# The first layer's softmax division by way of DRAM, and half of its bias product on GpSimd

## Chip, cores and metric

The kernel runs on one core of one Trainium2 chip. The metric is the device time of one execution in microseconds. The kernel before takes 1226.16 us (median of 3 runs, 1225.27 to 1228.61).

## What is computed

The input is 32 images of 16 by 16 tokens with 256 channels, all in float32. Two layers follow each other, each of the form x = x + attention(groupnorm(x)). The change touches the first layer alone, which is shifted-window attention: 4 windows of 64 tokens an image, 16 heads of 16 channels.

```python
q = (xw @ Wq.T).reshape(-1, N, HEADS, d).transpose(0, 2, 1, 3)      # k alike, v with a bias
qn = q / jnp.maximum(jnp.linalg.norm(q, axis=-1, keepdims=True), 1e-12)   # kn alike
logits = jnp.einsum('bhnd,bhmd->bhnm', qn, kn) * scale
logits = logits + 16.0 * jax.nn.sigmoid(bias)
lg = jnp.where(mask[None, :, None], -jnp.inf, lg)
scores = jax.nn.softmax(logits, axis=-1)
o = jnp.einsum('bhnm,bhmd->bhnd', scores, v)
z = o @ Wo.T + bo
```

## The kernel before

In the code the first layer is `layer0`. It is a software pipeline over the 32 images, written out for each engine by itself. The helper `pipeline` takes a list of stages with lags: in step s an engine runs each stage of its list, in the list's order, for image s + lag. Engines meet only at semaphores, so each engine works through its list in order, and an instruction that waits holds up all behind it on that engine.

Steps 4 to 25 are a hardware loop (`Fori`) of 11 rounds with two steps in each; steps -6 to 3 and 26 to 32 are written out in full. So ahead of each even step from 4 to 24 each engine jumps: it enters the loop, or goes back to its top. It does not jump ahead of an odd step.

What a step does in the kernel before, with the lines of its profile:

- TensorE (PE): `scores` of image s into psG (L365, L372), `project_v` of s+1 (L408), `output` of s-1 (L422), `bounds` of s+1 into psG (L389, L396), `turn` of s+2 (L433), `sums` of s, the softmax's denominators (L443), `weigh` of s, the weights times v (L457), `project` of s+3 in two halves (L469), `groups` of s+4 (L484), `turn_c` of s+1 (L476), and `spread_sums` of s (L491), one matmul that spreads 64 columns of inverted sums over 512.
- ScalarE (ACT): two `exponent` halves from psG into the weights (L575), `copy_v` (L567), `copy_z` of s-1 (L582), `normalize` of s+3 (L615), `copy_qk` (L589, L592), `copy_o` (L600), two `square` halves of s+3 (L559), `copy_c` (L605).
- VectorE (DVE): `add_bias`, the product of the exponentials with the exponential of the bias, in two halves (L698), `unit_qk` (L778), two `take_max` (L771), `invert_sums` (L681), `spread_blocks` (L686), statistics (L786, L793 to L717), two `norms` (L705), `outputs` of s (L676), which divides by the sums, and then `seeds` and `roots` (L727 to L763), a Newton iteration for reciprocal roots: 3 small instructions and then 9, nearly all of them waiting for the one in front. L763 is the last of them and writes `shift`.
- GpSimd (POOL): only `residual` of s-1, four additions into X (L828). The queue of SyncE (SP) issues the load of image s+6 (L301).

`newton` counts the nine instructions of `roots`, `biased` the bias products, `sums_done` and `r_done` the sums and their inverses, `o_out` the weighted values copied out, `o_done` the divided ones that `output` waits for. ebias, the weights and rdx (which holds the spread inverses) lie in SBUF; psG, psA and psE are PSUM.

## Time and profile before

| | before |
|---|---|
| median of 3 runs | 1226.16 us |
| profiled execution | 1223.74 us |
| its span | 1222.0 us |
| PE busy | 1153.9 us (94%) |
| DVE busy | 945.0 us (77%) |
| ACT busy | 639.0 us (52%) |
| POOL busy | 209.5 us (17%) |

The profiled execution took 1223.74 us, of which the span of the engines' instructions is 1222.0 us. The first layer lies between 0 and about 537 us of the span; its 32 steps begin with the L365 matmuls. "Idle before" is time in which an engine had nothing running, and the name behind the arrow is what released it as far as the profile can tell.

### The profile page before, as it was taken

The page shows a single profiled execution, that of the slowest core. Times are in us where ns is not written, and L with a number is a line of the kernel's source. Part 1 is how long each engine was busy: PE and PEld are TensorE (multiplying, and loading weights), DVE is VectorE, ACT ScalarE, POOL GpSimd, SP SyncE. Part 2 cuts the span into 40 slices and gives each one's busy share as a digit, 9 for nine tenths or more (in the row PEclk, how much of TensorE's full clock was granted, in tenths as well). Part 3 has the DMA queues.
Part 4 walks back from the last instruction along what each step waited for, and adds up shares of the span by engine and source line. Part 5 has one row for each costly group of instructions (what it writes and reads, how often), then busy time and mean ns, then how long its engine had stood idle before and what let it go on. Part 6 is the DMA issues. An engine that isn't in the chain of part 4 may idle for free.

```text
span 1222.0 us, 50870 instructions
## 1 busy us (share of the span) xinstructions
PE 1153.9 (94%) x21404; PEld 842.1 (69%) x21404; DVE 945.0 (77%) x1687; ACT 639.0 (52%) x1051; POOL 209.5 (17%) x271
## 2 busy tenths in 40 slices
PE   6899999999999999958899999999999999999983
PEld 3677777777777777736677777777777777777752
DVE  5588888888888898744577878787787878778753
ACT  4365566666566665422555555555555555555540
POOL 0001111111111111120212212221221222222120
PEclk9799999999999999988999999999999999999987
DMA  2000000000000000010023122222312222231222
GB/s 90 17 21 21 20 17 17 17 17 17 17 17 17 17 10 3 4 40 1 11 54 71 41 65 44 61 45 60 70 40 65 44 61 45 59 69 40 66 45 70
DMA packets 180189, 46.04 MB, mean 38 GB/s; under 512 B 146308, under 2 KB 179350, under 8 KB 180118
## 3 DMA queue, kind: packets, MB, share of 16 engines
q1 hardware_dynamic: 178056, 43.76, 15.2%
q10 hardware_dynamic: 2064, 1.26, 0.4%
q8 instruction: 56, 0.92, 0.3%
q14 instruction: 13, 0.11, 0.0%
HBM read 27.56 MB, written 17.30 MB: 37 GB/s over the span
## 4 chain that ended last, share of the span: by engine, by line
PE 44%; DVE 6%; issue 3%; SPq 0%; ACT 0%; DMA 0%; POOL 0%; POOLq 0%; DVEq 0%
PE psG L1063 14%; PE psA L1105 8%; PE psA L1121 6%; PE psG L1085 6%; PE psE L1154 5%; PE psA L1133 5%; DVE of L1261 3%; DVE sums L1256 2%; PE psG L1072 2%; DVE cm L1230 1%; PE psE L1144 1%; DMA sums<-totals 0%; SPq L1012 0%; ACT probs L1176 0%; POOL probs L1292 0%
## 5 line engine op out<-in xcount | busy, mean ns | idle before, releaser
L1230 DVE TENSOR_REDUCE cm<-psG 128x4 f32<-128x1024 f32 (+1 forms) x192 | 235.0, 1224 | 132.2 <-PE psG L1085 132.2
L1176 ACT ACTIVATE probs<-psG 128x1024 f32<-128x1024 f32 x192 | 196.4, 1023 | 143.4 <-PE psG L1063 143.0
L1063 PE MATMUL psG<-stack 32*128 32x256 f32 (+1 forms) x2048 | 222.6, 345 | 9.7 <-DVE cm L1230 6.6
L1292 POOL TENSOR_SCALAR_AFFINE_SELECT probs<-probs 128x1024 f32<-128x1024 f32 x128 | 139.2, 1099 | 517.6 <-ACT probs L1176 517.6
L1072 PE MATMUL psG<-stack 32*128 32x256 f32 (+1 forms) x2048 | 220.1, 342 | 4.3 <-DVE cm L1230 2.4
L1063 PEld LDWEIGHTS psG<-stack 32*128 32x128 f32 x2048 | 152.5, 188 | 68.0 <-DVE cm L1230 27.6
L1072 PEld LDWEIGHTS psG<-stack 32*128 32x128 f32 x2048 | 149.8, 185 | 7.0 <-DVE cm L1230 3.3
L828 POOL TENSOR_TENSOR X<-X,probs 128x96 f32 (+5 forms) x128 | 64.8, 536 | 467.8 <-ACT probs L582 467.8
L1121 PE MATMUL psA<-xh,wqk 128*128 128x256 f32 x512 | 126.2, 391 | 5.5 <-DVE xh L1267 5.5
L469 PE MATMUL psA<-probs,xh 128*128 128x512 f32 x256 | 128.7, 630 | 1.9 <-ACT xh L615 1.6
L1256 DVE RECIPROCAL sums<-sums 128x128 f32<-128x128 f32 x128 | 115.7, 929 | 10.4 <-DMA sums<-totals 10.4
L1121 PEld LDWEIGHTS psA<-xh,wqk 128*128 128x128 f32 x512 | 95.6, 197 | 17.7 <-DVE xh L1267 6.2
L1190 ACT ACTIVATE stack<-psA,at_row,own 128x256 f32<-128x256 f32 x128 | 65.1, 561 | 68.7 <-DVE stack L1236 68.7
L1105 PE MATMUL psA<-probs,va 128*32 128x256 f32 (+1 forms) x2048 | 97.8, 332 | 0.9 <-POOL probs L1292 0.9
L575 ACT ACTIVATE probs<-psG 128x1024 f32<-128x1024 f32 x64 | 62.0, 1021 | 69.8 <-PE psG L372 69.8
L698 DVE TENSOR_TENSOR probs<-probs,ebias 128x1024 f32<-128x1024 f32 x64 | 77.9, 1220 | 13.4 <-ACT probs L575 13.2
L1105 PEld LDWEIGHTS psA<-probs,va 128*32 128x32 f32 x2048 | 57.8, 110 | 37.2 <-issue 14.3
L1154 PE MATMUL psE<-of,wo 128*128 128x256 f32 x256 | 67.4, 408 | 16.7 <-DVE of L1261 15.0
L559 ACT ACTIVATE probs<-psA 128x512 f32<-128x512 f32 x64 | 38.1, 597 | 84.3 <-PE psA L469 84.3
L771 DVE TENSOR_REDUCE cm<-psG 128x16 f32<-128x1024 f32 x64 | 75.3, 1219 | 7.6 <-PE psG L396 6.7
L469 PEld LDWEIGHTS psA<-probs,xh 128*128 128x128 f32 x256 | 44.6, 194 | 38.8 <-issue 36.2
L1154 PEld LDWEIGHTS psE<-of,wo 128*128 128x128 f32 x256 | 48.2, 198 | 30.6 <-DVE of L1261 24.2
(132 smaller groups left out, 1890.0 us busy)
## 6 DMA issues: line engine op xcount, KB each, us to landing
X<-in_xr SPq DMA_DIRECT2D x32, 256.0 KB, 2.7
scratch_heads<-ots SPq DMA_DIRECT2D x128, 64.0 KB
raw<-scratch_heads SPq DMA_DIRECT2D x32, 256.0 KB
sums<-totals SPq DMA_DIRECT2D x64, 128.0 KB
out<-X SPq DMA_DIRECT2D x32, 256.0 KB, 3.1
totals<-ots SPq DMA_DIRECT2D x128, 4.0 KB
probs<-in_wqk ACTq DMA_DIRECT2D x1, 512.0 KB, 4.4
wqk<-in_wqk SPq DMA_DIRECT2D x1, 512.0 KB, 3.6
```

The costliest lines, as they stand in the source:

```text
L469: last = nc.tensor.matmul(A[t][:], xh[i.k][:, c, t * P:(t + 1) * P], wqk[:, c, :], start=(c == 0), stop=(c == CT - 1))
L698: nc.vector.tensor_tensor(both, both, bias.unsqueeze(2).to_broadcast([P, 4, WINDOWS, WTOK]), ALU.mult).then_inc(biased, 1)
L771: nc.vector.reduce_max(cm[:, t, :].rearrange("p (r s) -> p r s", s=COL)[:, :, 0:SLOTS], banks.rearrange("p r (s k) -> p r s k", k=WTOK), A ...
L1063: last = nc.tensor.matmul(G[:, at:at + b.size], km[i.k][own_rows(r), o, e, b.keys_of(o) * P:(b.keys_of(o) + 1) * P], qm[i.k][own_rows(r), ...
L1072: nc.tensor.matmul(G[:, at:at + b.size], qm[j.k][own_rows(r), o, e, b.queries_of(o) * P:(b.queries_of(o) + 1) * P], km[j.k][own_rows(r), o ...
L1105: last = nc.tensor.matmul(A[0 if o else 2][COL * c:COL * (c + 1), to:to + b.size], va[i.k][:, b.keys_of(o), TILE_HEADS * o + 2 * r + e, :] ...
L1121: last = nc.tensor.matmul(A[o][:, n * TOKENS:(n + 1) * TOKENS], wqk[:, c, n * CH + o * P:n * CH + (o + 1) * P], xh[i.k][:, c, :], start=(c ...
L1154: last = nc.tensor.matmul(E[:, o * TOKENS:(o + 1) * TOKENS], wo[:, f, o * P:(o + 1) * P], of[:, f, :], start=(f == 0), stop=(f == CT - 1))
L1176: nc.scalar.activation(weights[i.k][:, b.weights_at:b.weights_at + 1024], G[:, 0:1024], ACT.Exp).then_inc(exp_done, 1)
L1230: nc.vector.reduce_max(slots, scores, AX_X).then_inc(max_done, 1)
L1256: nc.vector.reciprocal(piece, piece).then_inc(r_done, 1)
L1292: nc.gpsimd.affine_select(out=diagonal, in_=diagonal, compare_op=ALU.is_ge, fill=0.0, base=0, pattern=[[0, QUADS], [0, 2], [sign, P]], cha ...
```

## The change

The spreading of the inverted sums leaves TensorE and VectorE. `spread_blocks` and `spread_sums` are gone. SyncE's queue instead writes the 128x64 inverses to a DRAM buffer (`put_inverses`, 32 KB) and reads them back broadcast into rdx (`get_inverses`, 256 KB, each head's row to 16 partitions). `outputs` now reads rdx from SBUF, not from PSUM, waits for that read, and moves from the end of step s to the front of step s+1.

The second half of the bias product moves to GpSimd (`add_bias` in the gpsimd block, on weight columns 1024 to 2047). It waits for both exponentials and for `newton` of image s+3, that is for the `roots` that VectorE ran last. From step 30 on there is no such wait.

The orders change too: on TensorE `bounds` comes ahead of `output`, `weigh` ahead of `sums`, `turn_c` ahead of the second half of `project`; on ScalarE `normalize` comes ahead of `copy_z` and `copy_c` ahead of the second `square`.

```diff
--- before.py
+++ after.py
+    inverses = nc.dram_tensor("inverses", [2, P, WTOK], F32).ap()
...
+            def put_inverses(i):
+                wait_alone(sp, r_done, i.count(1))
+                wait_alone(sp, got[i.k], i.plus(-2).dmas(1))
+                sp.dma_start(inverses[i.k], rd[:, :]).then_inc(put[i.k], 16)
+
+            def get_inverses(i):
+                wait_alone(sp, put[i.k], i.dmas(1))
+                wait_alone(sp, o_done, i.plus(-1).count(1))
+                by_head = inverses[i.k].rearrange("(g u n) q -> g u (n q)", u=2, n=8)[:, 0]
+                sp.dma_start(rdx, by_head.unsqueeze(1).to_broadcast([8, DIM, 512])).then_inc(got[i.k], 16)
+
+            pipeline(sp, images, [(load, 6), (put_inverses, 0), (get_inverses, 0)], LAGS, once={-5: small_inputs, -4: regions})
...
             def sums(i):
 
-                wait(pe, biased, i.count(2))
                 wait(pe, z_out, i.plus(-1).count(2))
+                wait(pe, r_done, i.plus(-1).count(1))
                 for n in range(8):
...
             def weigh(i):
 
-                wait(pe, v_out, i.count(2))
-                if i.plus(1).among(images):
-                    wait(pe, v_out, i.plus(1).count(2))
+                for n in range(2):
+                    wait(pe, biased[n], i.count(1))
+                wait(pe, v_out, (i.plus(1) if i.plus(1).among(images) else i).count(2))
                 for o in range(CT):
...
-            def spread_sums(i):
-
-                wait(pe, rdx_done, i.count(1))
-                nc.tensor.matmul(E[:, :], spread, rdx, start=True, stop=True).then_inc(spread_done, 1)
-
-            pipeline(pe, images, [(scores, 0), (project_v, 1), (output, -1), (bounds, 1), (turn, 2), (table_read, 0), (sums, 0), (weigh, 0),
-                                  (lambda i: project(i, 0), 3), (groups, 4), (lambda i: project(i, 1), 3), (turn_c, 1),
-                                  (spread_sums, 0)], LAGS, once={-3: hide_early, -2: hide_late, -1: tabulate})
+            pipeline(pe, images, [(scores, 0), (project_v, 1), (bounds, 1), (output, -1), (turn, 2), (weigh, 0), (table_read, 0), (sums, 0),
+                                  (lambda i: project(i, 0), 3), (groups, 4), (turn_c, 1), (lambda i: project(i, 1), 3)], LAGS, once={-3: hide_early, -2: hide_late, -1: tabulate})
...
-                                   (copy_v, 1), (copy_z, -1), (normalize, 3), (copy_qk, 2), (bias_across, 1),
-                                   (copy_o, 0), (lambda i: square(i, 0), 3), (lambda i: square(i, 1), 3), (bias_within, 1), (copy_c, 1)], LAGS, once={-3: rectify_early, -2: rectify_late, -1: open_table})
+                                   (copy_v, 1), (normalize, 3), (copy_z, -1), (copy_qk, 2), (bias_across, 1),
+                                   (copy_o, 0), (lambda i: square(i, 0), 3), (bias_within, 1), (copy_c, 1), (lambda i: square(i, 1), 3)], LAGS, once={-3: rectify_early, -2: rectify_late, -1: open_table})
...
             def outputs(i):
 
-                wait(dve, spread_done, i.count(1))
+                wait_alone(dve, got[i.k], i.dmas(1))
                 wait(dve, o_out, i.count(1))
                 raw = ot[:, :, :].rearrange("p o t -> p (o t)")
-                nc.vector.tensor_tensor(raw, E[:, :], raw, ALU.mult).then_inc(o_done, 1)
+                nc.vector.tensor_tensor(raw, rdx, raw, ALU.mult).then_inc(o_done, 1)
 
             def invert_sums(i):
                 wait(dve, sums_done, i.count(QUADS))
-                wait(dve, rdx_done, i.plus(-1).count(1))
+                wait_alone(dve, put[1 - i.k], i.plus(-1).dmas(1))
                 nc.vector.reciprocal(rd[:, :], E[:, 0:WTOK]).then_inc(r_done, 1)
 
-            def spread_blocks(i):
-                wait(dve, r_done, i.count(1))
-                wait(dve, spread_done, i.plus(-1).count(1))
-                nc.vector.tensor_tensor(rdx.rearrange("p (n q) -> p n q", q=WTOK), rd[:, :].unsqueeze(1).to_broadcast([P, 8, WTOK]),
-                                        block_of[:, :].unsqueeze(2).to_broadcast([P, 8, WTOK]), ALU.mult).then_inc(rdx_done, 1)
-
-            def add_bias(i, part):
-
-                wait(dve, exp_done, i.count(2, part + 1))
-                if part == 0:
-                    wait(dve, tab_in, 32)
-                    wait(dve, a_tab2, 4 * QUADS)
-                both = (weights[i.k][:, part * 1024:(part + 1) * 1024]
-                        .rearrange("p (n w q) -> p n w q", w=WINDOWS, q=WTOK))
-                bias = ebias[:, 2 * part:2 * part + 2, :, :].rearrange("p r o q -> p (r o) q")
+            def add_bias(i):
+
+                wait(dve, exp_done, i.count(2, 1))
+                wait(dve, tab_in, 32)
+                wait(dve, a_tab2, 4 * QUADS)
+                both = weights[i.k][:, 0:1024].rearrange("p (n w q) -> p n w q", w=WINDOWS, q=WTOK)
+                bias = ebias[:, 0:2, :, :].rearrange("p r o q -> p (r o) q")
                 nc.vector.tensor_tensor(both, both, bias.unsqueeze(2).to_broadcast([P, 4, WINDOWS, WTOK]),
-                                        ALU.mult).then_inc(biased, 1)
+                                        ALU.mult).then_inc(biased[0], 1)
...
-            pipeline(dve, images, [(lambda i: add_bias(i, 0), 0), (unit_qk, 2), (prepare_bounds, 2), (invert_table, 1), (lambda i: add_bias(i, 1), 0), (lambda i: take_max(i, 0), 1), (lambda i: take_max(i, 1), 1),
-                                   (invert_sums, 0), (spread_blocks, 0), (stats_next, -1), (stats_first, 5),
-                                   (variances, 4), (lambda i: norms(i, 0), 3), (lambda i: norms(i, 1), 3), (outputs, 0),
+            pipeline(dve, images, [(outputs, -1), (unit_qk, 2), (add_bias, 0), (prepare_bounds, 2), (invert_table, 1), (lambda i: take_max(i, 0), 1), (lambda i: take_max(i, 1), 1),
+                                   (invert_sums, 0), (stats_first, 5), (stats_next, -1),
+                                   (variances, 4), (lambda i: norms(i, 0), 3), (lambda i: norms(i, 1), 3), 
                                    (scale_ready, 4), (seeds, 4, 1), (roots, 4, 1)], LAGS,
...
-            pipeline(pool, images, [(residual, -1)], LAGS)
+            def add_bias(i):
+
+                wait(pool, exp_done, i.count(2))
+                if i.plus(3).among(images + 1):
+                    wait(pool, newton, i.plus(3).count(NEWTON))
+                if first(i):
+                    pool.wait_ge(tab_in, 32)
+                    pool.wait_ge(a_tab2, 4 * QUADS)
+                both = weights[i.k][:, 1024:2048].rearrange("p (n w q) -> p n w q", w=WINDOWS, q=WTOK)
+                bias = ebias[:, 2:4, :, :].rearrange("p r o q -> p (r o) q")
+                nc.gpsimd.tensor_tensor(both, both, bias.unsqueeze(2).to_broadcast([P, 4, WINDOWS, WTOK]),
+                                        ALU.mult).then_inc(biased[1], 1)
+
+            pipeline(pool, images, [(add_bias, 0), (residual, -1)], LAGS)
```

On VectorE, at the top of the hardware loop and just ahead of it (the same instructions stand ahead of a return to the top). Before, the roots' last instruction and the jump were followed by the bias product:

```order
L763 SCALAR_TENSOR_TENSOR shift<-gs,rs_y 128x2
L126 UNCONDITIONAL_BRANCH
L126 ISA
L698 TENSOR_TENSOR probs<-probs,ebias 128x1024 [waits a_tab2,tab_in,exp_done]
L93 ISA
L93 REGISTER_ALU [waits newton]
L778 TENSOR_TENSOR probs<-psA,rs_y 128x512 [waits turned]
L778 TENSOR_TENSOR probs<-psA,rs_y 128x512
L93 REGISTER_ALU
L698 TENSOR_TENSOR probs<-probs,ebias 128x1024 [waits exp_done]
```

And in the changed kernel:

```order
L754 SCALAR_TENSOR_TENSOR shift<-gs,rs_y 128x2
L126 UNCONDITIONAL_BRANCH
L126 ISA
L93 REGISTER_ALU [waits got1]
L675 TENSOR_TENSOR ot<-probs,ot 128x512 [waits o_out]
L93 ISA
L93 ISA [waits newton]
L769 TENSOR_TENSOR probs<-psA,rs_y 128x512 [waits turned]
L769 TENSOR_TENSOR probs<-psA,rs_y 128x512
L93 REGISTER_ALU
L689 TENSOR_TENSOR probs<-probs,ebias 128x1024 [waits a_tab2,tab_in,exp_done]
```

`outputs` (L675) has come to the front, with two SBUF inputs, and one bias product of two is left, behind `unit_qk` (L769).

On TensorE, the middle of a step in the loop, before:

```order
L422 MATMUL psE<-ot,probs 128x2x8x8 [waits o_done]
L422 MATMUL psE<-ot,probs 128x2x8x8 x7
L389 MATMUL psG<-stack 64x128 [waits gn_chain,exp_done,qk_out]
L389 MATMUL psG<-stack 64x128 x31
L396 MATMUL psG<-region_keys,region_queries 64x256 x16
L93 REGISTER_ALU
L433 MATMUL psA<-ident,probs 128x128 [waits qkn_done]
L433 MATMUL psA<-ident,probs 128x128 x7
L443 MATMUL psE<-probs 32x64 [waits z_out,biased]
L443 MATMUL psE<-probs 32x64 x31
L457 MATMUL psA<-probs,vw 32x64 [waits v_out]
L457 MATMUL psA<-probs,vw 32x64 x31
```

And in the changed kernel:

```order
L400 MATMUL psG<-stack 64x128 [waits gn_chain,exp_done,qk_out]
L400 MATMUL psG<-stack 64x128 x31
L407 MATMUL psG<-region_keys,region_queries 64x256 x16
L433 MATMUL psE<-ot,probs 128x2x8x8 [waits o_done]
L433 MATMUL psE<-ot,probs 128x2x8x8 x7
L93 REGISTER_ALU
L444 MATMUL psA<-ident,probs 128x128 [waits qkn_done]
L444 MATMUL psA<-ident,probs 128x128 x7
L468 MATMUL psA<-probs,vw 32x64 [waits v_out,biased1,biased0]
L468 MATMUL psA<-probs,vw 32x64 x31
L454 MATMUL psE<-probs 32x64 [waits r_done,z_out]
L454 MATMUL psE<-probs 32x64 x31
```

`bounds` (L400) now comes directly behind `project_v`, `output` (now L433) behind it, and `weigh` (L468) is the one that waits for both bias products.

## Rows read from the trace of the kernel before

**Rows 1.** Timeline of PE, one step: start us, length us, engine, line, operation.

```profile
255.76 1.53 PE L365 MATMUL psG<-stack 32*64 32x64 f32 x124
...
259.39 2.05 PE L422 MATMUL psE<-ot,probs 128*128 128x128 f32 x16
261.37 1.19 PE L389 MATMUL psG<-stack 32*64 32x128 f32 x63
...
262.73 1.10 PE L433 MATMUL psA<-ident,probs 128*128 128x128 f32 x8
263.75 1.10 PE L443 MATMUL psE<-probs 128*32 128x64 f32 x64
...
267.64 1.96 PE L469 MATMUL psA<-probs,xh 128*128 128x512 f32 x4
269.44 0.38 PE L476 MATMUL psG<-ident,cm 128*128 128x128 f32 x2
269.66 1.02 PE L491 MATMUL psE<-probs 128*128 128x512 f32 x2
270.74 1.53 PE L365 MATMUL psG<-stack 32*64 32x64 f32 x124
...
285.62 1.53 PE L365 MATMUL psG<-stack 32*64 32x64 f32 x124
```

**Rows 2.** Timeline of ACT, the same step and the next.

```profile
257.65 1.94 ACT L575 ACTIVATE probs<-psG 128x1024 f32<-128x1024 f32 x2 [2.02 <-PE psG L372]
...
272.71 1.94 ACT L575 ACTIVATE probs<-psG 128x1024 f32<-128x1024 f32 x2 [2.20 <-PE psG L372]
```

**Rows 3.** Timeline of DVE, the same step and the next.

```profile
259.25 0.15 DVE L763 SCALAR_TENSOR_TENSOR shift<-gs,rs_y 128x2 f32<-128x2 f32 x1
259.34 1.23 DVE L698 TENSOR_TENSOR probs<-probs,ebias 128x1024 f32<-128x1024 f32 x1
260.48 1.28 DVE L778 TENSOR_TENSOR probs<-psA,rs_y 128x512 f32<-128x512 f32 x2
261.68 1.22 DVE L698 TENSOR_TENSOR probs<-probs,ebias 128x1024 f32<-128x1024 f32 x1
...
270.27 0.69 DVE L705 TENSOR_REDUCE rs<-probs 128x32 f32<-128x512 f32 x1 [0.94 <-ACT probs L559]
...
271.47 0.22 DVE L727 SCALAR_TENSOR_TENSOR rs<-rs 128x66 f32<-128x66 f32 x1
...
274.14 0.15 DVE L763 SCALAR_TENSOR_TENSOR shift<-gs,rs_y 128x2 f32<-128x2 f32 x1
274.75 1.23 DVE L698 TENSOR_TENSOR probs<-probs,ebias 128x1024 f32<-128x1024 f32 x1 [0.46 <-ACT probs L575]
```

**Rows 4.** L828, the last image: count, duration ns min/median/max, forms.

```profile
L828 POOL TENSOR_TENSOR X<-X,probs x4: 249/383/785, 534.4 to 535.9; 128x96 f32<-128x96 f32 x2, 128x288 f32<-128x288 f32 x1, 128x32 f32<-128x32 f32 x1
```

**Rows 5.** L1261, all of the second layer, columns alike.

```profile
L1261 DVE TENSOR_TENSOR of<-raw,sums x32: 691/1116/1205, 624.3 to 1214.1; 128x512 f32<-128x512 f32 x32
```

**Rows 6.** Timeline of POOL and DVE around one L1261 (second layer).

```profile
623.81 1.10 POOL L1292 TENSOR_SCALAR_AFFINE_SELECT probs<-probs 128x1024 f32<-128x1024 f32 x1
624.34 1.11 DVE L1261 TENSOR_TENSOR of<-raw,sums 128x512 f32<-128x512 f32 x1
```

**Rows 7.** DMA issues: engine, operation, count, KB each, median us to landing.

```profile
X<-in_xr SPq DMA_DIRECT2D x32, 256.0 KB, 2.7
...
ebias<-probs ACTq DMA_DIRECT2D x2, 64.0 KB, 2.2
```

**Rows 8.** Timeline of all engines at the end of the first layer.

```profile
528.17 0.56 DVE L681 RECIPROCAL rd<-psE 128x64 f32<-128x64 f32 x1 [1.30 <-PE psE L443]
...
531.42 2.05 PE L422 MATMUL psE<-ot,probs 128*128 128x128 f32 x16 [0.78 <-DVE ot L676]
533.51 0.84 ACT L582 ACTIVATE probs<-psE,bz 128x256 f32<-128x256 f32 x2 [3.85 <-PE psE L422]
534.42 1.68 POOL L828 TENSOR_TENSOR X<-X,probs 128x288 f32<-128x288 f32 x4 [6.00 <-ACT probs L582]
```

26 lines of the change are left out of this document (9 added, 17 removed).

## Prediction

> **What bounds the kernel now.** The first thing to read is the timeline of TensorE over one step [rows 1], starts only, since the matmuls overlap. Scores start at 255.76, 270.74 and 285.62: two steps in 29.86 us, 14.93 each, and each block of matmuls starts as the last one's ends. In the first layer's loop TensorE shows no pause, so time taken out of its list is won, as long as nobody else becomes late. The pieces that I need, as differences of starts: scores and project_v together 3.63 (255.76 to 259.39), output 1.98, bounds 1.36, turn 1.02, then sums, weigh, the first half of project and groups together 3.89 (263.75 to 267.64), the second half of project 1.80, turn_c 0.22, spread_sums 1.08 (269.66 to 270.74).
>
> Then VectorE [rows 3]. From the second project's start (267.64) it goes by ScalarE's square to the second L705 at 270.27 (2.63 us), and from seeds at 271.47 to the end of L763, the last of the roots, at 274.29 (2.82); between them stands outputs (L676). The next thing to see is the difference of two neighbouring steps. In the first, L698 starts at 259.34, 0.06 before L763 ends. In the second VectorE is idle for 0.46 us and L698 starts at 274.75. The row blames the exponential, but its first half, which is what L698 waits for, was done by about 273.7 [rows 2], before L763 started. What lies between is the jump to the top of the loop. So in every even step of the loop VectorE comes 0.46 us late to what follows the roots. Before, this costs nothing, since sums has slack.
>
> Last, who can disturb whom in SBUF. L1261 in the second layer multiplies two SBUF tiles of 128x512 on VectorE. Alone it takes 691 ns, the minimum; the median is 1116 [rows 5]. The timeline shows the reason: GpSimd's L1292 runs from 623.81 to 624.91, L1261 starts at 624.34 and ends at 625.45, 0.54 after GpSimd [rows 6]. So VectorE stood still until GpSimd's whole instruction was done, and then did its 512 elements. The Trainium skill, "SBUF — State Buffer", section "Who interferes with whom", states this as an exclusive lock on a shared pair of ports, which the one that starts first keeps for a whole instruction. By that rule a VectorE instruction with one SBUF input isn't touched; the rule speaks against this change, and the row agrees with its first part.
>
> **The change, part by part.** I count from x, the start of the second half of project in the step before; the steady period is x to x. T is the start of scores.
>
> 1. *TensorE's list.* spread_sums goes: -1.08. T is now x + 1.80. But bounds moved ahead of output, and bounds overwrites the psG that the exponentials read. They start T + 1.89 (255.76 to 257.65) and take 1.94 [rows 2], so bounds can start at T + 3.83 plus about 0.12 for the signal, 3.95, where TensorE arrives at T + 3.63. The new wait is 0.32. By TensorE alone a step is 14.93 - 1.08 + 0.32 = 14.2. I take weigh's arrival from it: T + 3.95 + 1.36 + 1.98 + 1.02 = T + 8.31 = x + 10.1. From weigh to the next x: 3.89 + 0.22 = 4.11.
>
> 2. *spread_blocks* and one half of add_bias leave VectorE (the half at 261.68 is 1.22 long [rows 3]). VectorE isn't what TensorE waits for before, so this alone is worth nothing.
>
> 3. *The roots.* Without outputs ahead of them, seeds wait for L705's end: 0.69 + 0.03. L763 ends at x + 2.63 + 0.72 + 2.82 = x + 6.17. Call this u.
>
> 4. *GpSimd's product.* The trace has none of this size. From 32 elements in 249 ns and 288 in 785 undisturbed [rows 4] an element costs 2.09 ns, so 1024 elements cost 2.32 us. The lower bound is L1292's 1.10 us for as many elements with one input [rows 6]; I take 2.32, from the same operation with two inputs. With 1.10 the even steps below are 1.22 us shorter and the odd ones 0.1, some 15 us in all (1218). The upper bound is the 383 ns of the 96-element pieces taken per element, 4.1, fixed share and all; it would put 1.8 us on each step. I keep it for the range with little weight, since the 288 elements rule it out (they would take 1.15). The Trainium skill, "GPSIMD Engine Reference", section "Elementwise — side-by-side cycle accounting", gives about 2.6 cycles an element for two inputs, by which it would be an estimated 2.2 us and the sum below some 2 us less.
>
> 5. *Odd steps, and steps written out: VectorE first.* outputs starts at about u - 0.06 as L698 did, and ends at u + 0.62 by L1261's 0.69 undisturbed. It has two SBUF inputs now. GpSimd's product, released at u, stands until then and ends 2.32 - 0.15 later (0.15 is what L1261 had behind it before it was stopped, 0.69 - 0.54), at u + 2.79. unit_qk reads PSUM and one small SBUF tile. No row here shows such an instruction against GpSimd; I take it as running meanwhile, since only its second input is in SBUF, and price the contrary as a rival. add_bias, two SBUF inputs, would be ready at u + 1.7 and is held until u + 2.79, then takes 1.08 more: u + 3.87. With 0.1 for signals weigh may start at x + 10.1 to x + 10.2, just as TensorE arrives. The period is 10.17 + 4.11 = 14.3, against a mean of 14.93 before: -0.63.
>
> 6. *Even steps of the loop: GpSimd first.* After the jump outputs cannot start before u + 0.46. GpSimd already sits at its wait for newton, and starts 0.07 after a release (534.35 to 534.42 [rows 8]). It holds SBUF until u + 2.39. outputs ends 0.54 later, at u + 2.93. TensorE's output needs it, and turn and weigh stand behind output: it starts at x + 6.17 + 2.93 + 0.06 = x + 9.16, not at x + 7.1, and weigh at + 1.98 + 1.02 = x + 12.16. (The bias half ends at u + 2.93 - 0.09 + 1.20 + 1.23 = u + 5.27 = x + 11.45, hidden under it.) The period is 12.16 + 4.11 = 16.27: +1.34.
>
> 7. *The two transfers.* By the nearest rows, a write of 64 KB landed in 2.2 us and a read of 256 KB from DRAM in 2.7 [rows 7]: 4.9 with both. The inverses are ready about x - 1.4 (weigh and sums 1.93 behind W, invert 0.55 after), so rdx is there near x + 3.7 with the queue's own delays, and outputs wants it at x + 6.1. Hidden by 2.4 us a step. The loads of X are issued behind the read and have a whole step. At the layer's end nothing hides them: from the start of the last L681 to output it was 3.25 us (528.17 to 531.42 [rows 8]); now 0.55 + 4.9 + 0.69 + 0.1 = 6.2, and sums stand behind weigh and GpSimd's 2.32 instead of VectorE's 1.2. That is 3 + 2, of which the two last steps, free of VectorE work behind them, give something back. I take +4, between +2 and +6.
>
> The sum: 11 even steps x 1.34 = +14.7; 11 odd steps and 7 written-out full ones x -0.63 = -11.3; end +4. Together +7.4. Against the profiled 1223.7 us this is 1231.1; the median of the runs stands 2.4 above the profiled one, so I predict 1233.5.
>
> **Rivals.**
>
> *VectorE is never the one held* (0.17): the jump is faster in the new code, or GpSimd takes the ports more than 0.46 us after its release. For it: nothing in the trace shows a two-input product of GpSimd issued against a VectorE one at the same moment. Against: the 0.46 against the 0.07. All 29 steps then win 0.63, the end costs 4: -14, 1212. This is the case on the other side, and it decides at u + 0.46.
>
> *GpSimd first in the odd steps too* (0.09): if the wait for the transfer delays outputs by over 0.15 us. Then 11 more steps move from 14.30 to 16.27, +21.7: 1255.
>
> *unit_qk is held as well* (0.06), having an SBUF input. By the rule of the same page it isn't. Where VectorE goes first, unit_qk would start at u + 2.79 and add_bias end 1.2 later than above, 18 steps x 1.25 = +22: 1256.
>
> *The transfers are late* (0.04): from 7.3 us for both on, each microsecond costs one a step. With 8 us, 29 x 0.7 = +20: 1253.
>
> *Nothing nets out* (0.04), some cost and gain sized otherwise: 1226.
>
> **How the numbers follow.** The main case has 0.60. Its own range is 1228 to 1239: the even steps by 0.3 (3 us), the others by 0.2 (4 us), the end by 2. What a measurement can tell from no change is 0.3%, 3.7 us. The main case is slower than that in 0.8 of its weight, the same in 0.17. With the rivals: slower 0.48 + 0.09 + 0.06 + 0.04 = 0.67, faster 0.17 + 0.02 = 0.19, same 0.14. The range 1211 to 1248 leaves out the cases around 1255 and half of the faster one's low side.
>
> **What would show it.** Scores' starts alternating near 14.3 and 16.3 us in the loop. In even steps GpSimd's product 2.3 us long, then outputs with over 2 us on the clock, and TensorE idle by some 2 us before output, released by VectorE. In odd steps outputs of 0.7, a GpSimd product of about 2.9, and add_bias of over 2 us. TensorE idle 0.3 before bounds. No wait for a transfer before step 31, and 5 us of it there. What would make me wrong: equal steps, a GpSimd product of 3 us or more undisturbed, or VectorE waiting for a DMA inside the loop.

## The result, and the profile after

The changed kernel takes 1265.68 us (median of 4 runs, 1255.7 to 1273.61), the kernel before 1227.38 us on the same chip (4 runs, 1225.27 to 1228.95). The ratio is 1.031, 95% interval 1.022 to 1.040. The forecast was slower, and it was slower, but 1265.7 lies outside the range of 1211 to 1248: the cost is 38 us where 7 were forecast.

The profiled execution of the changed kernel took 1271.29 us, 5.6 more than the median. Its span is 1269.2 us against 1222.0, 47.2 more, so the parts below add up to more than the 38. Cut at the first scores of a step, it divides like this:

| stretch | before | after | difference |
|---|---|---|---|
| start to step 4 | 120.0 | 124.2 | +4.2 |
| steps 4 to 25, the hardware loop | 329.7 | 361.4 | +31.7 |
| steps 26 to 30 | 71.1 | 68.3 | -2.8 |
| step 31 to the end | 701.1 | 715.3 | +14.2 |

The first view is the timeline of TensorE, as in [rows 1], for steps 14 to 16.

```profile
287.68 1.53 PE L376 MATMUL psG<-stack 32*64 32x64 f32 x124
...
289.42 1.97 PE L419 MATMUL psA<-wv,xh 128*64 128x128 f32 x32
291.64 1.19 PE L400 MATMUL psG<-stack 32*64 32x128 f32 x63 [0.26 <-ACT probs L580]
...
295.24 2.05 PE L433 MATMUL psE<-ot,probs 128*128 128x128 f32 x16 [2.17 <-DVE ot L675]
...
298.10 1.10 PE L468 MATMUL psA<-probs,vw 128*32 128x64 f32 x64
...
304.05 1.53 PE L376 MATMUL psG<-stack 32*64 32x64 f32 x124
...
312.56 1.10 PE L468 MATMUL psA<-probs,vw 128*32 128x64 f32 x64 [0.31 <-DVE probs L689]
...
320.33 1.12 PE L376 MATMUL psG<-stack 32*64 32x64 f32 x81 [1.75 <-issue]
323.09 0.96 PE L376 MATMUL psG<-stack 32*64 32x64 f32 x41 [1.64 <-issue]
...
324.51 3.68 PE L419 MATMUL psA<-wv,xh 128*64 128x128 f32 x32
```

Step 14 (even) is 16.37 long. `output` (L433) comes 2.17 us late and the row names VectorE's `outputs`. Step 15 shows only 0.31 ahead of `weigh`. Then the scores of step 16 start at 320.33, 1.75 us after TensorE ran dry, and stop once more for 1.64, both times on "issue": nothing that the profile shows was waited for. After these pauses L419 takes 3.68 us in place of 1.97. VectorE and GpSimd in the same steps, with the counterparts of [rows 3]:

```profile
292.06 0.15 DVE L754 SCALAR_TENSOR_TENSOR shift<-gs,rs_y 128x2 f32<-128x2 f32 x1
292.29 2.35 POOL L832 TENSOR_TENSOR probs<-probs,ebias 128x1024 f32<-128x1024 f32 x1 [8.88 <-DVE shift L754]
292.61 2.58 DVE L675 TENSOR_TENSOR ot<-probs,ot 128x512 f32<-128x512 f32 x1 [0.40 <-issue]
295.11 1.28 DVE L769 TENSOR_TENSOR probs<-psA,rs_y 128x512 f32<-128x512 f32 x2
296.31 1.21 DVE L689 TENSOR_TENSOR probs<-probs,ebias 128x1024 f32<-128x1024 f32 x1
...
308.52 0.68 DVE L675 TENSOR_TENSOR ot<-probs,ot 128x512 f32<-128x512 f32 x1
308.68 2.75 POOL L832 TENSOR_TENSOR probs<-probs,ebias 128x1024 f32<-128x1024 f32 x1 [8.51 <-DVE shift L754]
309.12 1.28 DVE L769 TENSOR_TENSOR probs<-psA,rs_y 128x512 f32<-128x512 f32 x2
310.32 2.19 DVE L689 TENSOR_TENSOR probs<-probs,ebias 128x1024 f32<-128x1024 f32 x1
```

This is the alternation that the prediction described. In the even step the jump costs VectorE 0.40, GpSimd is first, and `outputs` lasts until 295.19, 0.55 after GpSimd's end. In the odd step `outputs` is first (0.68), and then L689 is the one held. L769, with one input in PSUM, takes 1.28 in both.

What the prediction didn't have shows in the windows, one line a step (steps 14, 15, 16 and 18), with the busy time of TensorE, its weight loads, VectorE, ScalarE and GpSimd, and then TensorE's granted clock, the DMA engines' share and GB/s:

```profile
287.67:304.05 16.38, 13.95 (x422) 10.83 (x421) 13.62 (x30) 9.09 (x17) 4.06 (x5) 1.00 0.12 33
304.05:320.33 16.28, 14.00 (x421) 10.84 (x421) 13.40 (x32) 9.76 (x18) 4.46 (x5) 1.00 0.15 36
320.33:338.54 18.21, 16.57 (x421) 13.08 (x421) 11.03 (x29) 8.61 (x16) 4.54 (x5) 0.81 0.13 34
...
354.68:372.69 18.01, 15.58 (x421) 12.46 (x421) 13.62 (x30) 9.20 (x17) 4.06 (x5) 0.91 0.12 30
```

The second line is an odd step of 16.28: 14.5 and the 1.75 of pause at its end. The third has a clock of 0.81, which means a part of the step at 1.2 GHz in place of 2.4. And the page's table of DMA queues has one line that changed, the fetching of instructions, first before and then after:

```profile
q8 instruction: 56, 0.92, 0.3%
```

```profile
q8 instruction: 83, 1.36, 0.4%
```

Each packet is a block of 16 KB of instructions. 27 more are three bursts of nine, and their times in the trace begin at 217.0, 315.9 and 415.5, each 0.6 to 0.7 us after TensorE's sequencer, which runs ahead of the matmuls, has jumped back to the top of the loop (216.36, 315.30 and 414.76). In the kernel before there is none between 145 and 448 us, that is from the first round, which brings the loop's code in, to the end of the last. So the loop's instructions, once fetched, normally stay on the chip; in the changed kernel they are now and then fetched anew.

### The profile page after: what moved, and what is told of

It reads as the page before. It is cut to its first block, busy times and chain, and to the rows that moved or that the text cites. A ratio compares the mean times of both kernels' runs of the same rounds, so it can differ in the third digit from the quotient of the medians.

```text
span 1269.2 us, 50942 instructions
## 1 busy us (share of the span) xinstructions
PE 1148.0 (90%) x21340; PEld 850.2 (67%) x21340; DVE 926.2 (73%) x1620; ACT 641.4 (51%) x1051; POOL 282.0 (22%) x303
## 4 chain that ended last, share of the span: by engine, by line
PE 43%; DVE 6%; issue 3%; SPq 1%; ACT 0%; DMA 0%; POOL 0%; POOLq 0%; DVEq 0%
PE psG L1067 13%; PE psA L1109 7%; PE psA L1125 6%; PE psG L1089 5%; PE psE L1158 5%; PE psA L1137 4%; DVE of L1265 3%; DVE sums L1260 2%; PE psG L1076 2%; DVE cm L1234 1%; PE psE L1148 1%; DMA sums<-totals 0%; SPq L1016 0%; ACT probs L1180 0%; SPq L1020 0%
## 5 line engine op out<-in xcount | busy, mean ns | idle before, releaser
L1180 ACT ACTIVATE probs<-psG 128x1024 f32<-128x1024 f32 x192 | 196.6, 1024 | 143.3 <-PE psG L1067 142.9
L832 POOL TENSOR_TENSOR probs<-probs,ebias 128x1024 f32<-128x1024 f32 x32 | 82.3, 2573 | 344.2 <-DVE shift L754 212.3
L433 PE MATMUL psE<-ot,probs 128*128 128x128 f32 x512 | 72.3, 299 | 30.2 <-DVE ot L675 30.2
L433 PEld LDWEIGHTS psE<-ot,probs 128*128 128x128 f32 x512 | 65.7, 208 | 37.1 <-DVE ot L675 34.4
L762 DVE TENSOR_REDUCE cm<-psG 128x16 f32<-128x1024 f32 x64 | 75.0, 1211 | 11.2 <-PE psG L407 11.2
L1109 PEld LDWEIGHTS psA<-probs,va 128*32 128x32 f32 x2048 | 57.8, 110 | 37.2 <-issue 14.3
L419 PE MATMUL psA<-wv,xh 128*64 128x128 f32 x1024 | 74.5, 301 | 7.6 <-issue 7.6
```

Of the source, the lines that this page charges most:

```text
L433: last = nc.tensor.matmul(dst[:, t], wo[:, f, o * P:(o + 1) * P], ot[:, f, t * P:(t + 1) * P].rearrange("p (ww rr c) -> p ww rr c", ww=2, ...
L832: nc.gpsimd.tensor_tensor(both, both, bias.unsqueeze(2).to_broadcast([P, 4, WINDOWS, WTOK]), ALU.mult).then_inc(biased[1], 1)
L1109: last = nc.tensor.matmul(A[0 if o else 2][COL * c:COL * (c + 1), to:to + b.size], va[i.k][:, b.keys_of(o), TILE_HEADS * o + 2 * r + e, :] ...
L1180: nc.scalar.activation(weights[i.k][:, b.weights_at:b.weights_at + 1024], G[:, 0:1024], ACT.Exp).then_inc(exp_done, 1)
```

## The experiments

Fifteen kernels were run, each timed against the kernel before on its own chip (in the four groups of runs its medians were 1241.52, 1230.6, 1233.42 and 1225.5 us; the first and the third are of one chip at two times). Lengths of steps and loops are those of one profiled execution each. The theory: the prediction's steps are right in the loop, and what it left out are re-fetched instructions with the lower clock behind them. The rivals: the held `outputs`, the product or the transfers cost more than was counted. Each expectation spells out what they mean for its run, and in the later ones the letters stand for what they name there.

### Two tries to move the loop that moved nothing

```diff
                 pe.wait_ge(made, MADE)
+                for _ in range(20):                # and 128
+                    pe.nop(nofuse=True)
                 for q in range(HALF):
```

> The changed kernel with 20 empty instructions on TensorE ahead of its loop, nothing else. In the changed kernel TensorE's instruction blocks (16 KB each) are fetched again in the loop, nine of them every third round, from 217, 316 and 416 us on; before, none is fetched inside the loop. Its loop starts 17 instructions earlier than that of before. Theory A (where the loop lies against the 16 KB blocks decides whether it is fetched again): with the loop's start back at the old place there are no fetches in the loop, no odd step of 16 or 18 us, odd steps 14.5 and even ones 16.4, and the kernel takes about 1240 us (1234 to 1246). Rival B (the fetches come from TensorE's longer waits or from the traffic of the two transfers): the fetches stay, 1255 to 1273 us.

> The same with 128 empty instructions, half a block. Theory A: the loop's 1710 instructions end 128 further into the last block; either no fetches (about 1240 us) or more of them (every round, over 1280 us), in any case another pattern than nine blocks every third round. Rival B: unchanged, 1255 to 1273 us with the same fetches.

Measured 1271.67 us (pad20), ratio 1.025 (1.018 to 1.031), and 1270.08 (pad128), ratio 1.024 (1.017 to 1.031). The trace counts as many instructions up to each fetch as in the changed kernel, so the empty instructions didn't reach the instruction stream. These are two repeats of the changed kernel and say nothing on the loop's place. What they do show is that the fetches vary: four bursts (187.7 to 423.7 us) in one, three in the other, with a clean stretch from 311 to 435 in which steps are 14.46 and 16.37.

### GpSimd's product behind outputs

```diff
             def add_bias(i):                       # on GpSimd
                 if i.plus(3).among(images + 1):
-                    wait(pool, newton, i.plus(3).count(NEWTON))
+                    wait(pool, o_done, i.plus(-1).count(1))
```

> The changed kernel, but GpSimd's product waits for outputs of image s-1 (o_done) where it waited for the roots. Theory (in even steps GpSimd takes SBUF ahead of outputs): outputs is 0.7 us long in every step, TensorE waits for it no more, GpSimd's product ends 3.1 to 3.7 us after the roots and the bias half on VectorE is held until then; even steps 15.1 in place of 16.4, odd steps 14.5 to 14.7, 11 to 14 us less than the changed kernel's 1266, with the fetches as they are: about 1253. Rival (outputs is late for another reason, the rdx transfer): outputs still ends 2.9 us after the roots in even steps, no gain.

Measured 1238.1 us (hold_outputs), ratio 0.998 (0.995 to 1.001). The timeline of an even step:

```profile
304.75 0.69 DVE L675 TENSOR_TENSOR ot<-probs,ot 128x512 f32<-128x512 f32 x1 [0.40 <-issue]
305.53 2.36 POOL L832 TENSOR_TENSOR probs<-probs,ebias 128x1024 f32<-128x1024 f32 x1 [10.15 <-DVE ot L675]
306.56 2.41 DVE L689 TENSOR_TENSOR probs<-probs,ebias 128x1024 f32<-128x1024 f32 x1
```

The same jump of 0.40, but `outputs` is back to 0.69. Steps are 15.23 and 14.68, the loop 329.6, and no fetch and no halved clock falls into it. So the order of the two engines is what makes the even steps long, and the transfers don't. The fetches went as well, with not one TensorE instruction changed; the expectation had left them in.

### Both halves of the product on VectorE, transfers kept

```diff
-  pipeline(dve, images, [(outputs, -1), (unit_qk, 2), (add_bias, 0), ...
+  pipeline(dve, images, [(outputs, -1), (unit_qk, 2), (lambda i: add_bias(i, 0), 0), (lambda i: add_bias(i, 1), 0), ...
-  pipeline(pool, images, [(add_bias, 0), (residual, -1)], LAGS)
+  pipeline(pool, images, [(residual, -1)], LAGS)
```

> The changed kernel with both halves of the bias product on VectorE (behind unit_qk), none on GpSimd; the two transfers stay. Theory: no VectorE instruction is held by GpSimd; even steps 15.1 (the jump's 0.46 us and the longer VectorE list), odd ones 14.5, about 1253 us with the fetches as they are, 1228 without. Rival (the transfers cost the step): even steps stay at 16.4 and the kernel above 1260.

Measured 1236.99 (product_vector), ratio 0.997 (0.994 to 1.000), steps 15.29 and 14.67, loop 330.2, no fetches. The transfers by themselves cost nothing in the loop. At the end they do: from step 31 to the last `output` it is 18.1 us against 10.5, and 707.9 from step 31 on against 701.1.

### The product on GpSimd, without transfers

```diff
   # the kernel before without VectorE's second half, and on GpSimd the changed kernel's add_bias
...
-                wait(pe, biased, i.count(2))
+                for n in range(2):
+                    wait(pe, biased[n], i.count(1))
-  pipeline(pool, images, [(residual, -1)], LAGS)
+  pipeline(pool, images, [(add_bias, 0), (residual, -1)], LAGS)
```

> The kernel before with the second half of the bias product on GpSimd alone, held until the roots as in the change; sums are spread by TensorE, outputs stays ahead of the roots. Theory (the lock costs only because outputs, which TensorE wants early, stands behind the product): in even steps the VectorE half is about 3.4 us long on the clock, sums waits for nothing, steps 14.9, ratio 0.995 to 1.005. Rival (GpSimd's product costs in itself): over 1.01.

Measured 1228.05 (product_only), ratio 0.997 (0.994 to 1.000); steps 14.88 and 14.98, loop 329.8, no fetches. Each half of the change alone is harmless. The expectation had GpSimd first in the even steps and VectorE's half 3.4 us long. It came otherwise: VectorE's half is released by the first exponential, GpSimd's by the second, so VectorE is first in both kinds of steps (304.77 against 305.03, and 319.39 against 319.81). Its half keeps its 1.23, and GpSimd's product takes 3.19 and 3.03. So this run shows a product on GpSimd that costs nothing behind VectorE's, and not what one costs ahead of it; the loss is seen only where GpSimd starts ahead of `outputs`.

### VectorE's list rotated, so that the jump falls elsewhere

```diff
-  pipeline(dve, images, [(outputs, -1), (unit_qk, 2), (add_bias, 0), ..., (invert_sums, 0), (stats_first, 5), ..., (roots, 4, 1)], LAGS,
+  pipeline(dve, images, [(stats_first, 5), ..., (roots, 4, 1), (outputs, 0), (unit_qk, 3), (add_bias, 1), ..., (invert_sums, 1)], LAGS,
```

> The changed kernel with VectorE's list rotated, nothing else: it begins with the statistics of X and ends with outputs, unit_qk, add_bias, the maxima and invert_sums, so that VectorE jumps behind invert_sums and no more between the roots and outputs. Theory (the jump lets GpSimd take SBUF first in even steps): outputs is 0.7 us long and VectorE goes first in every step, even and odd steps both take 14.5 us (30.8 us a pair in the clean rounds of the changed kernel, 29.9 before), no fetches in the loop, and the kernel takes 8 to 12 us less than hold_outputs, 0.985 to 0.995 of before. Rival (GpSimd wins for another reason, by chance or with the parity of the buffers): even steps stay at 16.4, ratio over 1.01.

> The same rotation with both halves of the product on VectorE. Theory: steps of 14.4 to 14.5 as in rotate, since add_bias then ends 4.1 us behind the roots either way, and the layer's end some 2 us shorter, as GpSimd doesn't hold outputs of image 30; ratio 0.98 to 0.995. Rival (the product on GpSimd is worth its place): slower than rotate by 5 us or more.

Measured with the product on GpSimd (rotate) 1265.77, ratio 1.028 (1.020 to 1.035); with both halves on VectorE (rotate_vector) 1231.98, ratio 1.000 (0.997 to 1.004), steps 14.79 and 14.75, no fetches. An even step of the first:

```profile
302.12 0.69 DVE L675 TENSOR_TENSOR ot<-probs,ot 128x512 f32<-128x512 f32 x1
302.21 2.83 POOL L833 TENSOR_TENSOR probs<-probs,ebias 128x1024 f32<-128x1024 f32 x1 [8.90 <-DVE shift L754]
...
303.93 2.19 DVE L689 TENSOR_TENSOR probs<-probs,ebias 128x1024 f32<-128x1024 f32 x1
```

With the jump out of the way VectorE is 0.09 ahead of GpSimd, `outputs` is not held, and the even steps between bursts are 14.5 (the odd ones take 15.8 to 17.7 here, and 14.5 in a shifted version below). That should have won some 10 us in the loop. The kernel lost 35: five bursts of fetches in 11 rounds (101 packets on the page), and steps of up to 18.5 at them. TensorE waits only 0.6 us in a clean step here. So fetches don't need the alternating steps; they are a cost of their own. With both halves on VectorE the gain didn't come either: steps of 14.8 and not 14.5, a loop of 325.3 (4.4 less than before), and an end no shorter than with GpSimd (714.3 and 713.0 from step 31 on).

### TensorE made idle in the kernel before

```diff
             def output(i):
+                wait(pe, lingered, i.plus(1).count(1))
...
+            def linger(i):                         # on GpSimd
+                wait_alone(pool, lingered, i.plus(-1).count(1))
+                if not isinstance(i.pair, int) and i.k == 0:               # even steps of the loop
+                    wait_alone(pool, exp_done, i.count(2))
+                    nc.gpsimd.memset(spare[:, :], 0.0).then_inc(lingered, 1)   # 128x2048
+                else:
+                    nc.gpsimd.memset(spare[:, 0:1], 0.0).then_inc(lingered, 1)
```

> The kernel before, only that in the even steps of the loop output also waits for a GpSimd memset of 128x2048 that starts when the exponentials are done, which leaves TensorE idle for about 2.1 us there; no transfer and no product moved. Theory C (TensorE's idle time of over 2 us in each round brings both the new fetches of instructions and the halved clock): bursts of about nine 16 KB fetches appear in the loop and the clock halves in places; even steps 17.0 and some steps 1.7 longer still, over 1265 us on a chip where before takes 1227. Rival D (fetches come from the transfers' DMA traffic or the new code): no fetches, even steps 17.0, +23 us and no more.

Measured 1272.23 (before_idle), ratio 1.032 (1.025 to 1.039). Clean pairs are 15.0 and 17.13; there are three bursts (83 packets), and the clock is halved for 3.4 us at a time even where nothing is fetched. The loop is 376.2, 23 us above eleven clean pairs. A kernel without transfers or a product on GpSimd re-fetches too. (The added wait also puts three instruction records more ahead of TensorE's loop and two more into a round, so its code isn't quite at the old place.)

### Moving the loop against the blocks

Now with instructions that do reach the stream, small matmuls whose result is overwritten, on the rotated kernel:

```diff
                 pe.wait_ge(made, MADE)
+                for _ in range(32):                # 64, 96: 128 and 192 records
+                    nc.tensor.matmul(E[0:WTOK, 0:16], pick[:, 0, :], region_queries[:, 0:16], start=True, stop=True)
                 for q in range(HALF):
```

> The kernel with the rotated VectorE list, and 32 small matmuls more on TensorE once, ahead of the loop (64 instruction records of some 1,706 a round), which move the loop's instructions against the 16 KB blocks in which the trace shows TensorE's instructions being fetched. Theory A, the place of the loop against these blocks decides whether a round re-fetches: a loop of 6.7 blocks touches 7 blocks in about a third of all places and 8 in the rest, so that of shifts by 0, 64, 128 and 192 records at least one has no fetch inside the loop, even clock, steps of 14.5 us, a loop from step 4 to step 26 of 319 us and a ratio of 0.99 to 1.00, while the others re-fetch as the unshifted kernel does (loop 345 to 360, ratio 1.02 to 1.03). Rival B, the loop's timing decides: all three shifts re-fetch, with ratios of 1.02 to 1.03 and no relation to the shift.

> The same with 64 small matmuls (128 records). Theory A: one of the shifts by 64, 128 and 192 runs without fetches in the loop, with a loop of 319 us; rival B: this one re-fetches, loop 345 to 360 us, ratio 1.02 to 1.03.

> The same with 96 small matmuls (192 records). Theory A: one of the shifts by 64, 128 and 192 runs without fetches in the loop, with a loop of 319 us; rival B: this one re-fetches, loop 345 to 360 us, ratio 1.02 to 1.03.

| rotate, shifted by records | fetch packets | loop, us | time, us | ratio |
|---|---|---|---|---|
| 0 | 101 | 357.8 | 1265.77 | 1.028 (1.020 to 1.035) |
| 64 | 119 | 376.5 | 1283.7 | none given (1264.58 to 1312.43) |
| 128 | 146 | 392.0 | 1303.56 | 1.062 (1.054 to 1.069) |
| 192 | 57 | 321.4 | 1234.87 | 1.004 (1.000 to 1.008) |

The first row is of another chip than the others.

The same loop, at another place in the program, takes from 321 to 392 us. At a shift of 128, nine packets come after each of the ten jumps back, 90 in all: the loop's whole code is fetched anew each time. At 192 there is none from 157 us on, when the code has come in once, and every step from 6 to 25 is 14.5. That its time is no better than that of the kernel before has two reasons outside the loop: the first scores come at 69.1 us and not at 58.8, of which the matmuls themselves are 3.2, and the clock is low for 27.3 us up to there and not for 17.1; and the end is that of the other kernels with the transfers (713.0 from step 31 on). Two steps of the last one in windows:

```profile
320.62:335.15 14.53, 13.92 (x421) 10.83 (x420) 13.01 (x31) 9.24 (x17) 4.53 (x5) 1.00 0.15 39
335.15:349.67 14.52, 13.94 (x421) 10.82 (x421) 12.41 (x30) 9.11 (x17) 4.45 (x5) 1.00 0.15 38
```

### What was still open: does the shift cure the changed kernel?

The 96 matmuls now stand at the very head of TensorE's program, where it waits until 7.5 us anyway, on cleared operands:

```diff
+            pe.wait_ge(blanked, 1)
+            for _ in range(96):
+                nc.tensor.matmul(E[0:WTOK, 0:16], blank[:, :], blank[:, 0:16], start=True, stop=True)
             pe.wait_ge(c_avg, 16)
```

> The changed kernel itself with 96 small matmuls on cleared operands at the head of TensorE's program, where it waits for its first operands anyway (it starts at 7.5 us); they move the loop by 192 instruction records, the shift that rid the rotated kernel of its fetches. Theory A (the prediction's sum failed because it left out the re-fetch of TensorE's instructions and the halved clock behind it; VectorE's held operations are worth what was predicted): no fetch in the loop, no halved clock in it, steps 14.46 and 16.37 throughout, loop from step 4 to step 26 of 339 us in place of 361, a time some 22 us under the changed kernel's, ratio 1.012 to 1.020. Rival B (the fetches follow the alternation of short and long steps, or the transfers): fetches in the loop remain, loop near 360 us, ratio 1.025 to 1.035.

Measured 1252.29 (after_shift192), ratio 1.022 (1.016 to 1.027). That lies between the 1.012 to 1.020 of theory A and the 1.025 to 1.035 of B, and its interval reaches into both, so the time doesn't decide; the trace does. The page has 57 fetch packets, none in the loop from 151 us on, and the two steps below repeat unchanged from step 7 to 25:

```profile
326.72:341.18 14.46, 13.93 (x421) 10.84 (x421) 12.60 (x30) 9.16 (x17) 4.45 (x5) 1.00 0.15 39
341.18:357.55 16.37, 13.93 (x421) 10.82 (x420) 13.62 (x30) 9.09 (x17) 4.05 (x5) 1.00 0.12 34
```

The loop takes 343.1 us in place of 361.4. That is 18.3 of the 22 expected; the other 4 lie in steps 4 to 6, where the loop's code comes in for the first time and the clock is halved once.

> The kernel before with TensorE made idle for some 2 us in every second step (the run that re-fetched and took 1.032), shifted by 192 records as well. Theory A: the idle time stays (steps 15.0 and 17.1) but no fetch falls in the loop, so that it takes 353 us in place of 376, ratio 1.015 to 1.022. Rival B (a TensorE that stands idle re-fetches wherever its loop lies): fetches and halved clock remain, ratio 1.03.

Measured 1269.15 (idle_shift192), ratio 1.034 (1.030 to 1.039). Both theories are half right. No fetch is left in the loop from 154 us on (57 packets), but it takes 370.1 us and not 353, as most of the longer steps still take 18.6 us, and the windows show a lower clock in these and not in the ones of 17.13:

```profile
360.19:378.83 18.64, 16.45 (x422) 12.66 (x423) 13.41 (x33) 9.19 (x17) 3.53 (x6) 0.91 0.04 14
427.39:444.52 17.13, 14.94 (x422) 11.22 (x423) 13.39 (x33) 9.07 (x17) 3.55 (x6) 1.00 0.05 15
```

In TensorE's timeline the halved stretch begins right behind the idle time:

```profile
366.08 2.96 PE L430 MATMUL psE<-ot,probs 128*128 128x128 f32 x16 [2.19 <-POOL spare L844]
368.97 1.80 PE L396 MATMUL psG<-stack 32*64 32x128 f32 x64
```

[rows 1] have 2.05 and 1.19 for the same two. So here an idle time of 2.19 went with the lower clock by itself. The changed kernel's idle of 2.17 did not, in the clean steps above. But it did in its step 18, in the round behind a burst, at a time when nothing was fetched:

```profile
362.25 3.28 PE L433 MATMUL psE<-ot,probs 128*128 128x128 f32 x16 [2.17 <-DVE ot L675]
```

Why one does and the other doesn't, no run here tells.

> The kernel before, with nothing but 48 small matmuls (96 records) at the head of TensorE's program. By the estimate of where the loop starts in its 16 KB block (the first fetches of the trace), this puts it where the rotated kernel fetched most (its shift by 128). Theory A: fetches in nearly every round, steps up from 15.0, ratio 1.03 to 1.06, with no work of the loop changed. Rival B (timing decides): no fetches in the loop, as in the kernel before, ratio 1.00.

```diff
+            pe.wait_ge(blanked, 1)                 # the kernel before, otherwise untouched
+            for _ in range(48):
+                nc.tensor.matmul(E[0:WTOK, 0:16], blank[:, :], blank[:, 0:16], start=True, stop=True)
```

Measured 1316.6 (before_shift96), ratio 1.075 (1.069 to 1.081): the slowest kernel of all, with not one instruction of its loop changed. 146 fetch packets, a loop of 414.5 us, and these steps, with the start of the first of them in TensorE's timeline:

```profile
306.83:326.25 19.42, 15.70 (x423) 11.48 (x423) 13.42 (x33) 9.19 (x17) 1.70 (x4) 1.00 0.06 17
326.25:345.12 18.87, 16.90 (x424) 12.80 (x423) 13.52 (x33) 9.20 (x17) 1.70 (x4) 0.91 0.07 18
```

```profile
306.83 0.46 PE L370 MATMUL psG<-stack 32*64 32x64 f32 x25
309.48 1.29 PE L370 MATMUL psG<-stack 32*64 32x64 f32 x102 [2.19 <-issue]
...
312.94 1.53 PE L413 MATMUL psA<-wv,xh 128*64 128x128 f32 x23 [1.22 <-issue]
...
321.06 0.30 PE L462 MATMUL psA<-probs,vw 128*32 128x64 f32 x2 [0.32 <-issue]
```

TensorE stands for 2.19, 1.22 and 0.32 us on "issue", amid blocks of matmuls. I take this for what a missing instruction looks like in a profile; such pauses of over 0.4 us add up to 61.8 us in this loop, and the kernel before has one of 1.1 in its own. Its first scores come at 59.0 us, as in the kernel before (59.1): the matmuls at the head cost nothing by themselves.

### The version that these point to

The rotated list and the 192 records at the head together:

> The changed kernel with VectorE's list rotated, shifted by 192 records at the head of TensorE's program, where the 96 matmuls lie in its first wait. Theory A: no fetches in the loop, steps 14.52, loop 320 us (before: 330), first scores at 59 us and not 69, tail as in the rotated kernel (12 us longer than before): 1224 us on the chip of the first run, ratio 0.990 to 0.997. If the shift at the head moves the loop otherwise than the one ahead of the table: fetches, ratio 1.02 or more.

Measured 1229.59 (best), ratio 1.003 (1.001 to 1.005), above the 0.990 to 0.997 expected. The loop is as forecast (321.4, 8.3 less than before, steps of 14.5, no fetches). What was misjudged is outside: the first scores come at 62.8 and not at 59, steps 0 to 3 take 2.3 more, and from step 31 on it is 715.4, 14.3 more than before. That is 20 us against a gain of 8. The profiled execution is the longest of the ten, 6.3 above their median, which may be why the median is only 4 us above that of the kernel before. Three versions lie below the kernel before, and none by more than 0.3%, which is the limit of what can be told: the transfers with the whole product on VectorE (0.997), the product on GpSimd without transfers (0.997), and the product behind `outputs` (0.998).

## Why the prediction was wrong

*The loop's steps: right.* It had 14.3 for odd and 16.27 for even steps; clean ones are 14.46 and 16.37. GpSimd's product takes 2.35 (2.32 predicted), TensorE waits 0.26 before `bounds` (0.32) and 2.17 before `output` (2), `unit_qk` isn't held, the 0.40 of the jump decides who is first. The rival that VectorE would never be held fell, as did the one that `unit_qk` would be. hold_outputs and rotate show the cause by removing it in two ways. The Trainium skill, "SBUF — State Buffer", section "Who interferes with whom", held in all of this, where the prediction's "one SBUF input isn't touched" is what it says of products of two tensors and not of every VectorE instruction: whichever engine came first kept SBUF for its whole instruction, 2.58 for a 0.69 in one order and 2.75 for a 2.35 in the other, and the instruction with a PSUM input went on. Eleven clean pairs would be 339.1 us, 9.4 more than before; the sum of steps 5 and 6 gives 7.8.

*The step that failed is the sum itself.* It took "In the first layer's loop TensorE shows no pause, so time taken out of its list is won" from the kernel before, and added the list's costs to a loop taken to be fed with instructions and clocked as there. What this left out was put at nothing, and it is the largest term: the loop took another 22.3 us (361.4 - 339.1). They show as ten pauses on "issue" of 1.1 to 1.9 us, 16.3 together (1.6 of it in the first round), stretches of 3.4 and 6.8 us at 1.2 GHz behind them, and a write of the inverses of 4.3 us beside one burst, where it takes 1.6 otherwise, after which `outputs` waited 1.41 us for its DMA. after_shift192 shows it for the changed kernel: the same loop without fetches is 18.3 us shorter. The ratio falls from 1.031 to 1.022, though the two intervals overlap. before_shift96 shows the size that it can reach: 85 us.

The forecast was +7.4 and the profiled spans are 47.2 apart. Of the 39.8 between them 22.3 are this term, 1.6 the loop's clean steps, and 10.2 the end. Most of the rest is the start: the first scores come 2.7 later, and steps 0 to 3 take 1.5 more where 2.5 less was forecast. In one of them TensorE pauses for 2.70 us on "issue", with 3.4 us of the halved clock at it. Kernels with the same TensorE list had their first scores anywhere from 58.5 to 62.0 us, so the 2.7 can't be put down to the change.

*Why the fetches come.* The loop is some 1,706 to 1,717 TensorE instruction records, and up to the first jump back of the kernel before 21 fetches come 257 records apart on average. So a block of 16 KB is about 256 records, and the loop 6.7 blocks. By where it begins it touches seven or eight blocks. At the two worst places nine blocks come in a round (90 in the ten rounds behind the first, at both), which is one more than the loop can touch. I take the ninth for the block behind the loop, fetched ahead; the trace doesn't say which block a packet holds. At a shift 64 records further none comes. This agrees with a store that holds eight, in which a loop of eight is pushed out by the ninth and a loop of seven is not. The Trainium skill, "Runtime: NRT & Kernel Launch", section "Instruction fetch mechanics", gives 128 KiB for this engine, first in, first out, in blocks of 16 KiB. It also says that a taken branch whose target is outside the current window of two such blocks forces a fetch. By that each jump back over 6.7 blocks would fetch; the kernel before makes ten of them from 145 to 448 us with no fetch, so here the measurement decides against the window and for the larger store. By the same section of the Trainium skill crossing a block's border is "mostly hidden". That fits the straight code of steps 26 to 30 in the kernel before, with 3.7 us of pauses for 16 blocks, and not the loop of before_shift96, with 61.8 for 97.

Place alone isn't all: rotate and rotate_vector have the same TensorE code at the same place, and one fetches in every second round while the other doesn't at all. The changed kernel and hold_outputs differ in the same manner, and but for some records the kernel before and before_idle. I take it that at these places the ninth block is fetched ahead or not by how the loop runs, but what tips it was not shown. It isn't the amount of TensorE's waiting: rotate has 0.6 us a clean step and fetches, rotate_vector 0.8 and doesn't. The four shifts of one kernel, and the kernel before at two places, are what is shown.

*The end: mis-sized.* +4 was predicted, +14.2 came. Most of it is the transfers and not GpSimd: from step 31 to the last `output` it is 18 to 22 us in all versions with them, also with the whole product on VectorE, and 10 to 12 in all without. The chain of waits at the end of the first layer, as [rows 8]:

```profile
553.21 0.56 DVE L680 RECIPROCAL rd<-psE 128x64 f32<-128x64 f32 x1 [0.88 <-PE psE L454]
...
558.66 2.34 POOL L832 TENSOR_TENSOR probs<-probs,ebias 128x1024 f32<-128x1024 f32 x1 [4.96 <-ACT probs L580]
559.12 2.42 DVE L675 TENSOR_TENSOR ot<-probs,ot 128x512 f32<-128x512 f32 x1 [4.64 <-DMA probs<-inverses]
...
561.60 3.78 PE L433 MATMUL psE<-ot,probs 128*128 128x128 f32 x16 [5.03 <-DVE ot L675]
...
568.54 0.56 DVE L680 RECIPROCAL rd<-psE 128x64 f32<-128x64 f32 x1 [5.86 <-PE psE L454]
...
569.12 0.32 SPq L307 DMA_DIRECT2D inverses<-rd  x1
...
570.57 0.60 SPq L313 DMA_DIRECT2D probs<-inverses  x1
...
574.29 0.69 DVE L675 TENSOR_TENSOR ot<-probs,ot 128x512 f32<-128x512 f32 x1 [4.59 <-DMA probs<-inverses]
575.04 3.38 PE L433 MATMUL psE<-ot,probs 128*128 128x128 f32 x16 [6.66 <-DVE ot L675]
```

The last image went as predicted: 6.5 us from the inverse to `output` (6.2), and both transfers 5.2 (4.9, of which the 2.2 were read from a row that goes from SBUF to SBUF and not to DRAM). What the prediction gave back, "the two last steps, free of VectorE work behind them", was a second bill: image 30 waits 4.64 for its transfers as well, its `outputs` arrives 0.46 after GpSimd has begun, is held for 2.42, and with TensorE idle for 5.0 and 6.7 us `output` then runs at half the clock (3.78 and 3.38 in place of 2.05). From step 31 to the last `output` it is 21.1 us against 10.5. The other 3.6 lie behind it, in the second layer, where the executions of these kernels differ by 5.6 among themselves (689.8 to 695.4), so no cause can be given for them. And the transfers show earlier than the prediction's "No wait for a transfer before step 31": `outputs` waits 4.89 us for them in step 30, of which 1.47 reach TensorE, and over 1 us in each of the three steps of the loop that a burst falls into.

## To carry to other kernels

When two engines are released by the same event and share SBUF, ask who is ahead by tenths of a microsecond, and look for a jump in one of their lists: 0.4 us decided over 2 us a step here. When a loop on TensorE comes near the size of the instruction store, look at the page's instruction queue and at pauses on "issue" after every edit, also one that doesn't touch the loop; if the packet count has risen, move the loop by some tens of instructions before judging the edit. And count a transfer's latency at a pipeline's end once for every image that is no longer covered, together with what the idle time does to TensorE's clock.

## What the runs showed of the hardware

- A loop of 6.7 instruction blocks ran 321, 358, 377 and 392 us at four places in the program, and the untouched kernel before went from 329.7 to 414.5.
- Re-fetching in every round cost 7.7 us a round on average (85 over 11 rounds), mostly in pauses of up to 2.5 us amid matmuls.
- Empty instructions on TensorE left no trace in the instruction stream; small matmuls did, at 33 ns each (3.2 us for 96 ahead of the table).
- An idle time of TensorE of 2.2 us was followed by 3.4 us at half the clock in some steps and not in others, in one and the same kernel.
- GpSimd's product of 1,024 columns with two SBUF inputs takes 2.35 us alone, and 2.75 where VectorE's 0.68 began 0.16 ahead of it.
